# Other start addresses for TensorE's stationary operands, in an attention and expert kernel in split float32

## The chip, the cores and the metric

The kernel runs on one core of one Trainium2 chip. The metric is device time in microseconds from launch to end. The profile is of one further execution; its span runs from the first to the last instruction.

## The reference

The input `x` is 32 sequences of 256 rows of 256 numbers. A bias chosen by an integer per sequence is added to `x` to make the queries; `side` serves as keys and as values:

```python
q = query + braak_embed[braak_stages][..., None]
attn = softmax(einsum('bsd,btd->bst', q, key))
o = einsum('bst,btd->bsd', attn, value)
```

The attention output is normalised by its root mean square and a weight (call it `t`, 8192 rows of 256), and goes through eight experts that share dense weights and differ by low-rank terms. The two best experts of each row count:

```python
h1 = t @ w1.T + SCALING * einsum('etr,efr->etf', t·a1, b1)      # F = 1024, rank 16 per expert
h3 = t @ w3.T + SCALING * einsum('etr,efr->etf', t·a3, b3)
act = silu(h1) * h3
out_e = act @ w2.T + SCALING * einsum(..., act·a2, b2)
out = x + sum over e of weights[t, e] * out_e
```

All of it is float32.

## The kernel before, in words

Float32 products are made of three matmuls. Every operand is split into a high part, a copy rounded to the type float32r, and a low part, what is left; `product` (lines 1190 to 1195) issues high x high, high x low, low x high. A matmul has a stationary operand, which a weight load (PEld in the profile) brings into the array, and a moving one, which streams past it. In `nc.tensor.matmul(dst, w, x)` the first operand, `w`, is stationary and the second, `x`, moving. The profile's names put them the other way round, moving first: `bank<-t_hi,w1T_hi` has `t_hi` moving and `w1T_hi` stationary. Each matmul has its own weight load of 128 columns.

The first stage, up to about 195 us, goes through the 32 sequences one by one: transposes of queries and keys (line 1246, plain fp32, `ident` moving), scores (line 1266 and after: `qT` stationary, `kT` moving, 256 columns), softmax, transposes of the probabilities (line 1297), `attend` (`value` stationary, `probT` moving, 256 columns), and `gate` (line 1319, plain fp32, the same `oT` tile as stationary and moving, 136 columns; its rows are 160 words apart). Between these, `weight_job` (line 1239) transposes the weights, and ScalarE and VectorE write their high and low parts. For `w2_in` and `a2_in` the stationary operand of the transpose takes one word in eight, starting 0 to 7 words in; for the others it is contiguous. The value parts are written by ScalarE (high) and GpSimd (low, line 552), the query and key parts by ScalarE (high) and VectorE (low, lines 857 and 859).

The second stage takes 16 tiles of 512 rows, each in eight chunks of 128 of the F = 1024 columns. Of a tile `pe_tile` (line 1440) issues `low_rank` (`a13T` stationary, 12 matmuls), and by chunk `first_expert` (18: `w1T`, `w3T`, `b1T`, `b3T` stationary), `second_expert` (6: `b1T`, `b3T`), `down_z` (6: `a2T`), all with 512 columns moving. `down_y` (12 per chunk: the activation parts `s` stationary, `w2T` moving) and `finish_y` (12 per tile: `z` stationary, `b2T` moving) have 256 columns. In a tile other than the first the order is low_rank, second_expert, down_z, first_expert, first_expert, second_expert, down_z, first_expert, then down_y twice and finish_y. The order is written out by hand, and semaphores join the engines.

SBUF tensors are laid one behind another in the order in which they are made (lines 72 to 175); `early` ones share their space with the late ones. Two pads, `pad_w` of 352 words and `pad_t` of 304, set where the rest begins. The size of all tensors between `ident` and the small vectors is a multiple of 512 bytes, and so is that of every large tensor of both stages, so all parts of the split operands start on multiples of 512 bytes.

Of the kernel before, what the change touches and what calls it, by code (L numbers as in the profile page):

```python
# [25 lines left out]
F32R = mybir.dt.float32r  # L26
# [5 lines left out]
P = 128  # L32
BATCH, S, D = 32, 256, 256
F, E, R = 1024, 8, 16
STAGES = 6
ER = E * R
SC = S // P
DC = D // P
FC = F // P
# [13 lines left out]
def adaln_moe_ffn(nc, x, side, itok, embed, norm_w, w1, w3, w2, gate_w, a1, b1, a3, b3, a2, b2, out):  # L53
    ctx = ExitStack()
    with ctx:
# [6 lines left out]
        def sb(stack, name, shape, dt=F32):  # L62
            return stack.enter_context(nc.sbuf_tensor(name, shape, dt))
# [7 lines left out]

        sb(ctx, "pad_w", [P, 352])
        ident = sb(ctx, "ident", [P, P])
        def split(name, shape, stack=ctx):
            return sb(stack, name + "_hi", shape, F32R), sb(stack, name + "_lo", shape, F32R)

        w1T = split("w1T", [P, DC, F])
        w3T = split("w3T", [P, DC, F])
        w2T = split("w2T", [P, FC, D])
        a2T = split("a2T", [P, FC, ER])  # L80
        a13T = split("a13T", [P, DC, 2, ER])
        b1T = split("b1T", [ER, F])
        b3T = split("b3T", [ER, F])
        b2T = split("b2T", [ER, D])
        rank_key = sb(ctx, "rank_key", [P, E])
        stage_id = sb(ctx, "stage_id", [STAGES, 1])
        gateT = sb(ctx, "gateT", [P, DC, E])
# [25 lines left out]

        rt = [sb(ctx, f"rt{k}", [P, KT]) for k in range(2)]

        sb(ctx, "pad_t", [P, 304])
        O_STRIDE = P + 32
        GATE = slice(P, P + E)
        early = ExitStack()
# [11 lines left out]
        x_in = [sb(early, f"x_in{k}", [P, SC, D]) for k in range(RING)]  # L131
        kv = [sb(early, f"kv{k}", [P, SC, D]) for k in range(RING)]
        q = [sb(early, f"q{k}", [P, SC, D]) for k in range(2)]
        qT = [split(f"qT{k}", [P, DC * S], early) for k in range(2)]
        kT = [split(f"kT{k}", [P, DC * S], early) for k in range(2)]
        prob = [sb(early, f"prob{k}", [P, SC, S]) for k in range(2)]
        value = [split(f"value{k}", [P, SC, D], early) for k in range(2)]
        probT = [split(f"probT{k}", [P, SC * S], early) for k in range(2)]
        oT = [sb(early, f"oT{k}", [P, DC, SC, O_STRIDE]) for k in range(2)]
        gram_diag = sb(early, "gram_diag", [P, SC, P])  # L140
        embed_in = sb(early, "embed_in", [STAGES, S])
# [1372 lines left out]
```

## Time and profile before

| | |
|---|---|
| median of 3 runs | 1311.74 us (1311.71 to 1311.76) |
| the profiled execution | 1313.57 us |
| its span | 1311.8 us |
| matmuls busy | 1304.6 us, 99% of the span, 7278 instructions |
| weight loads busy | 1143.5 us, 87% |
| VectorE / ScalarE / GpSimd busy | 844.0 / 527.0 / 250.0 us |
| granted TensorE clock | 1.00 |

A matmul's busy time in these views is its latency from start to modelled end, and the next starts before that end. The rate of a stream of matmuls is read from their starts. A weight load is shown with its own start and length. A line "x4" in the order of time merges four instructions that follow each other; its start is that of the first.

### The profile page before, as it was taken

To read this page: it belongs to the slowest core of one execution; us is meant where nothing else is said; L and a number is where in the kernel's file an instruction comes from. 1 tells how busy PE (TensorE), PEld (TensorE's weight loads), DVE (VectorE), ACT (ScalarE), POOL (GpSimd) and SP (SyncE) were. 2 spreads that over 40 slices of the span, in tenths; PEclk is the share of its full clock that TensorE was granted. 3 is DMA by queue.
4 is the path that set the end of the run, shared out by engine and by line. 5 is a ranking of instruction groups with operands and counts; after the bars stand their busy time and mean duration, and the time that the engine had idled before them with its cause. 6 is when DMAs were issued, how large, how long until landed. Compare 5 with 4: busy or idle time off the path is not lost.

```text
span 1311.8 us, 18591 instructions
## 1 busy us (share of the span) xinstructions
PE 1304.6 (99%) x7278; PEld 1143.5 (87%) x7278; DVE 844.0 (64%) x1558; ACT 527.0 (40%) x991; POOL 250.0 (19%) x213
## 2 busy tenths in 40 slices
PE   8999999999999999999999999999999999999998
PEld 8999998888888888888888888888888888888887
DVE  6776656756666576656675577557675666565556
ACT  6776653333343333333343334333333343243332
POOL 2656640202011020202020202011020202020200
PEclk9999999999999999999999999999999999999999
DMA  9454810020202020101102020202020101102000
GB/s 293 133 157 147 228 56 33 2 72 1 73 2 73 1 73 1 58 17 28 47 2 73 1 72 2 73 0 73 2 72 1 57 17 34 41 1 72 0 17 16
DMA packets 73583, 69.56 MB, mean 53 GB/s; under 512 B 7050, under 2 KB 64792, under 8 KB 73368
## 3 DMA queue, kind: packets, MB, share of 16 engines
q1 hardware_dynamic: 72924, 68.11, 17.2%
q8 instruction: 57, 0.93, 0.3%
q10 hardware_dynamic: 572, 0.28, 0.1%
q14 instruction: 30, 0.25, 0.1%
HBM read 51.27 MB, written 17.10 MB: 52 GB/s over the span
## 4 chain that ended last, share of the span: by engine, by line
PE 98%; ACT 1%; DVE 1%; DMA 0%; issue 0%; ACTq 0%; DVEq 0%
PE bank L1193 31%; PE bank L1194 31%; PE bank L1195 31%; PE bank L1319 2%; PE bank L1246 2%; PE bank L1297 1%; PE bank L1239 1%; DMA kv<-in_fside_BxSxS 0%; ACT prob L654 0%; PE bank L1284 0%; ACT kT_hi L638 0%; ACT qT_hi L637 0%; DVE q L850 0%; DVE x_out L1137 0%; PE bank L1326 0%
## 5 line engine op out<-in xcount | busy, mean ns | idle before, releaser
L1065 DVE TENSOR_TENSOR act_a<-silu_a,bank 128x512 f32<-128x512 f32 x128 | 87.6, 685 | 212.4 <-PE bank L1195 195.8
L745 ACT ACTIVATE br_hi<-act_br 128x512 fp32r<-128x512 f32 x128 | 80.9, 632 | 188.4 <-DVE act_br L1076 188.4
L738 ACT ACTIVATE silu_b<-bank 128x512 f32<-128x512 f32 x128 | 76.2, 596 | 187.9 <-PE bank L1195 187.1
L581 POOL TENSOR_TENSOR t_lo<-t_in,t_hi 128x512 fp32r<-128x512 f32 x32 | 40.6, 1290 | 553.2 <-ACT t_hi L725 553.2
L1193 PE MATMUL bank<-w2T_hi,s_hi 128*128 128x256 f32 x512 | 145.2, 284 | 0.0
L1195 PE MATMUL bank<-w2T_hi,s_lo 128*128 128x256 f32 x512 | 145.0, 283 | 0.0
L1194 PE MATMUL bank<-w2T_lo,s_hi 128*128 128x256 f32 x512 | 144.9, 283 | 0.0
L1073 DVE TENSOR_TENSOR act_b<-silu_b,bank 128x512 f32<-128x512 f32 x128 | 87.9, 687 | 81.6 <-PE bank L1195 80.6
L734 ACT ACTIVATE silu_a<-bank 128x512 f32<-128x512 f32 x128 | 75.7, 591 | 135.4 <-PE bank L1195 135.3
L600 POOL TENSOR_TENSOR v_lo<-v_full,v_hi 128x512 fp32r<-128x512 f32 x64 | 94.5, 1510 | 137.2 <-ACT v_hi L730 137.2
L1086 DVE TENSOR_TENSOR br_lo<-act_br,br_hi 128x512 fp32r<-128x512 f32 x128 | 104.7, 818 | 5.6 <-ACT br_hi L745 3.1
L1080 DVE TENSOR_TENSOR act_s<-act_a,act_br 128x512 f32<-128x512 f32 x128 | 103.2, 806 | 4.4
L1193 PE MATMUL bank<-t_hi,w1T_hi 128*128 128x512 f32 x256 | 100.2, 391 | 0.0
L1193 PEld LDWEIGHTS bank<-w2T_hi,s_hi 128*128 128x128 f32 x512 | 98.1, 192 | 2.4
L1194 PE MATMUL bank<-t_lo,w1T_hi 128*128 128x512 f32 x256 | 100.0, 391 | 0.0
L1076 DVE TENSOR_TENSOR act_br<-act_b,rho 128x512 f32<-128x512 f32 x128 | 97.2, 759 | 4.4
L1194 PEld LDWEIGHTS bank<-w2T_lo,s_hi 128*128 128x128 f32 x512 | 98.1, 192 | 2.2
L1193 PE MATMUL bank<-v_hi,b1T_hi 128*128 128x512 f32 x256 | 99.8, 390 | 0.0
L1194 PE MATMUL bank<-v_lo,b1T_hi 128*128 128x512 f32 x256 | 99.7, 390 | 0.0
L1194 PE MATMUL bank<-v_lo,b3T_hi 128*128 128x512 f32 x256 | 99.7, 390 | 0.0
L1193 PE MATMUL bank<-v_hi,b3T_hi 128*128 128x512 f32 x256 | 99.7, 389 | 0.0
L1195 PE MATMUL bank<-v_hi,b1T_lo 128*128 128x512 f32 x256 | 99.7, 389 | 0.0
(197 smaller groups left out, 3255.9 us busy)
## 6 DMA issues: line engine op xcount, KB each, us to landing
x_in<-in_x SPq DMA_DIRECT2D x32, 256.0 KB, 3.7
t_scratch<-oT SPq DMA_DIRECT2D x32, 256.0 KB, 2.5
t_in<-t_scratch SPq DMA_DIRECT2D x16, 512.0 KB
x_out<-in_x SPq DMA_DIRECT2D x16, 512.0 KB, 3.9
kv<-in_fside_BxSxS SPq DMA_DIRECT2D x31, 256.0 KB, 3.4
out<-x_out SPq DMA_DIRECT2D x30, 256.0 KB, 3.9
rho<-scale_scratch SPq DMA_DIRECT2D x16, 256.0 KB
rstd<-scale_scratch SPq DMA_DIRECT2D x16, 256.0 KB
```

The costliest lines, as they stand in the source:

```text
L600: nc.gpsimd.tensor_tensor(v_lo[k][:, :], v_full[k][:, :], f32(v_hi[k][:, :]), ALU.subtract).then_inc(v_lo_ready, 1)
L734: nc.scalar.activation(silu_a[j % 2][:, :], h1_bank[j % 2][:, :], ACT.Silu).then_inc(silu_a_ready, 1)
L738: nc.scalar.activation(silu_b[:, :], h1_bank[j % 2][:, :], ACT.Silu).then_inc(silu_b_ready, 1)
L745: nc.scalar.activation(br_hi[j % 2][:, :], act_br[j % 2][:, :], ACT.Copy).then_inc(br_hi_ready, 1)
L1065: nc.vector.tensor_tensor(act_a[j % 2][:, :], silu_a[j % 2][:, :], h3_bank[j % 2][:, :], ALU.mult).then_inc(act_a_ready, 1)
L1073: nc.vector.tensor_tensor(act_b[:, :], silu_b[:, :], h3_bank[j % 2][:, :], ALU.mult).then_inc(act_b_ready, 1)
L1076: nc.vector.tensor_tensor(act_br[j % 2][:, :], act_b[:, :], rho[c % 2][:, :], ALU.mult).then_inc(act_br_ready, 1)
L1080: nc.vector.tensor_tensor(act_s[j % 2][:, :], act_a[j % 2][:, :], act_br[j % 2][:, :], ALU.add).then_inc(act_s_ready, 1)
L1086: low = nc.vector.tensor_tensor(br_lo[j % 2][:, :], act_br[j % 2][:, :], f32(br_hi[j % 2][:, :]), ALU.subtract)
L1193: nc.tensor.matmul(dst, w_hi, x_hi, start=start, stop=False, skip_group_check=not grouped)
L1194: nc.tensor.matmul(dst, w_hi, x_lo, start=False, stop=False, skip_group_check=not grouped)
L1195: return nc.tensor.matmul(dst, w_lo, x_hi, start=False, stop=stop, skip_group_check=not grouped)
```

## The change

It puts gaps of 8 to 80 words ahead of the high and low parts of the stationary operands and takes 256 words from the second pad. `split` gets a parameter for the gap ahead of each part. No instruction, wait or transfer is added or taken away.

```diff
--- before.py
+++ after.py
@@ -71,17 +71,22 @@
 
         sb(ctx, "pad_w", [P, 352])
         ident = sb(ctx, "ident", [P, P])
-        def split(name, shape, stack=ctx):
-            return sb(stack, name + "_hi", shape, F32R), sb(stack, name + "_lo", shape, F32R)
-
-        w1T = split("w1T", [P, DC, F])
-        w3T = split("w3T", [P, DC, F])
-        w2T = split("w2T", [P, FC, D])
-        a2T = split("a2T", [P, FC, ER])
-        a13T = split("a13T", [P, DC, 2, ER])
-        b1T = split("b1T", [ER, F])
-        b3T = split("b3T", [ER, F])
-        b2T = split("b2T", [ER, D])
+        def split(name, shape, stack=ctx, gaps=(0, 0)):
+            parts = []
+            for part, words in zip(("_hi", "_lo"), gaps):
+                if words:
+                    sb(stack, name + part + "_gap", [P, words])
+                parts.append(sb(stack, name + part, shape, F32R))
+            return tuple(parts)
+
+        w1T = split("w1T", [P, DC, F], gaps=(8, 8))
+        w3T = split("w3T", [P, DC, F], gaps=(8, 24))
+        w2T = split("w2T", [P, FC, D], gaps=(80, 0))
+        a2T = split("a2T", [P, FC, ER], gaps=(64, 8))
+        a13T = split("a13T", [P, DC, 2, ER], gaps=(8, 8))
+        b1T = split("b1T", [ER, F], gaps=(8, 8))
+        b3T = split("b3T", [ER, F], gaps=(8, 8))
+        b2T = split("b2T", [ER, D], gaps=(8, 0))
         rank_key = sb(ctx, "rank_key", [P, E])
         stage_id = sb(ctx, "stage_id", [STAGES, 1])
         gateT = sb(ctx, "gateT", [P, DC, E])
@@ -113,7 +118,7 @@
 
         rt = [sb(ctx, f"rt{k}", [P, KT]) for k in range(2)]
 
-        sb(ctx, "pad_t", [P, 304])
+        sb(ctx, "pad_t", [P, 48])
         O_STRIDE = P + 32
         GATE = slice(P, P + E)
         early = ExitStack()
@@ -131,11 +136,11 @@
         x_in = [sb(early, f"x_in{k}", [P, SC, D]) for k in range(RING)]
         kv = [sb(early, f"kv{k}", [P, SC, D]) for k in range(RING)]
         q = [sb(early, f"q{k}", [P, SC, D]) for k in range(2)]
-        qT = [split(f"qT{k}", [P, DC * S], early) for k in range(2)]
-        kT = [split(f"kT{k}", [P, DC * S], early) for k in range(2)]
+        qT = [split(f"qT{k}", [P, DC * S], early, ((8, 8), (16, 16))[k]) for k in range(2)]
+        kT = [split(f"kT{k}", [P, DC * S], early, ((80, 0), (0, 0))[k]) for k in range(2)]
         prob = [sb(early, f"prob{k}", [P, SC, S]) for k in range(2)]
-        value = [split(f"value{k}", [P, SC, D], early) for k in range(2)]
-        probT = [split(f"probT{k}", [P, SC * S], early) for k in range(2)]
+        value = [split(f"value{k}", [P, SC, D], early, ((64, 16), (24, 8))[k]) for k in range(2)]
+        probT = [split(f"probT{k}", [P, SC * S], early, ((16, 0), (0, 0))[k]) for k in range(2)]
         oT = [sb(early, f"oT{k}", [P, DC, SC, O_STRIDE]) for k in range(2)]
         gram_diag = sb(early, "gram_diag", [P, SC, P])
         embed_in = sb(early, "embed_in", [STAGES, S])
```

## Rows read from the trace of the kernel before

**Rows 1.** The page's first part: busy us, share of the span, instructions.

```profile
PE 1304.6 (99%) x7278; PEld 1143.5 (87%) x7278; DVE 844.0 (64%) x1558; ACT 527.0 (40%) x991; POOL 250.0 (19%) x213
```

**Rows 2.** The page's fourth part: the chain by engine, then by line.

```profile
PE 98%; ACT 1%; DVE 1%; DMA 0%; issue 0%; ACTq 0%; DVEq 0%
PE bank L1193 31%; PE bank L1194 31%; PE bank L1195 31%; PE bank L1319 2%; PE bank L1246 2%; PE bank L1297 1%; PE bank L1239 1%; DMA kv<-in_fside_BxSxS 0%; ACT prob L654 0%; PE bank L1284 0%; ACT kT_hi L638 0%; ACT qT_hi L637 0%; DVE q L850 0%; DVE x_out L1137 0%; PE bank L1326 0%
```

**Rows 3.** Stretches: us, busy us (count) by engine, clock, DMA share, GB/s.

```profile
30.00:195.00 165.00, 164.93 (x1369) 162.32 (x1369) 108.76 (x317) 113.19 (x286) 94.34 (x90) 1.00 0.51 149
195.00:1307.00 1112.00, 1112.00 (x5722) 955.20 (x5721) 714.73 (x1197) 396.21 (x667) 146.92 (x105) 1.00 0.11 32
```

**Rows 4.** Matmuls in order of time: start us, us, engine, line, operands.

```profile
878.24 0.40 PE L1193 MATMUL bank<-t_hi,a13T_hi 128*128 128x512 f32 x1
...
898.67 0.28 PE L1193 MATMUL bank<-w2T_hi,s_hi 128*128 128x256 f32 x1
```

**Rows 5.** The same view from 902.98 us, and one weight load (PEld).

```profile
902.98 0.40 PE L1193 MATMUL bank<-v_hi,b1T_hi 128*128 128x512 f32 x1
...
903.45 0.39 PE L1195 MATMUL bank<-v_hi,b1T_lo 128*128 128x512 f32 x1
...
904.37 0.39 PE L1193 MATMUL bank<-s_hi,a2T_hi 128*128 128x512 f32 x1
...
902.98 0.19 PEld L1194 LDWEIGHTS bank<-v_lo,b1T_hi 128*128 128x128 f32 x1
```

**Rows 6.** Weight loads of transposes and gate in order of time.

```profile
126.66 0.47 PEld L1246 LDWEIGHTS bank<-ident,kv 128*128 128x128 f32 x4
127.09 1.00 PEld L1319 LDWEIGHTS bank<-oT 128*128 128x128 f32 x8
128.02 0.19 PEld L1193 LDWEIGHTS bank<-probT_hi,value_hi 128*128 128x128 f32 x1
```

**Rows 7.** Matmul groups by form, with their counts and mean latency.

```profile
L1193 PE MATMUL bank<-w2T_hi,s_hi 128*128 128x256 f32 x512 | 145.2, 284 | 0.0
...
L1193 PE MATMUL bank<-t_hi,w1T_hi 128*128 128x512 f32 x256 | 100.2, 391 | 0.0
...
L1193 PE MATMUL bank<-br_hi,a2T_hi 128*128 128x512 f32 x128 | 49.8, 389 | 0.0
...
L1193 PE MATMUL bank<-probT_hi,value_hi 128*128 128x256 f32 x128 | 39.0, 304 | 0.0
L1193 PE MATMUL bank<-kT_hi,qT_hi 128*128 128x256 f32 x124 | 37.5, 303 | 0.0
...
L1193 PE MATMUL bank<-t_hi,a13T_hi 128*128 128x512 f32 x64 | 25.2, 394 | 0.0
```

**Rows 8.** Groups of weight loads, and two groups that write the parts.

```profile
L1193 PEld LDWEIGHTS bank<-w2T_hi,s_hi 128*128 128x128 f32 x512 | 98.1, 192 | 2.4
...
L1193 PEld LDWEIGHTS bank<-v_hi,b1T_hi 128*128 128x128 f32 x256 | 48.1, 188 | 9.6
...
L552 POOL TENSOR_TENSOR value_lo<-kv,value_hi 128x512 fp32r<-128x512 f32 x32 | 41.4, 1293 | 80.4 <-ACT value_hi L648 80.4
...
L857 DVE TENSOR_TENSOR qT_lo<-bank,qT_hi 128x512 fp32r<-128x512 f32 x31 | 21.4, 691 | 16.3 <-ACT qT_hi L637 16.1
```

**Rows 9.** `w2_in` loads (first) and `w1_in`, `w3_in` ones; then in order.

```profile
L1239 PEld LDWEIGHTS bank<-ident,w_in x16: 186/189/193, 35.2 to 44.8; 128*128 128x128 f32 x16
...
L1239 PEld LDWEIGHTS bank<-ident,w_in x12: 139/140/142, 26.4 to 32.8; 128*128 128x128 f32 x12
...
38.47 0.53 PEld L1239 LDWEIGHTS bank<-ident,w_in 128*128 128x128 f32 x4
38.91 0.19 PEld L1193 LDWEIGHTS bank<-kT_hi,qT_hi 128*128 128x128 f32 x1
...
29.16 0.47 PEld L1239 LDWEIGHTS bank<-ident,w_in 128*128 128x128 f32 x4
29.60 0.42 PEld L1319 LDWEIGHTS bank<-oT 128*128 128x128 f32 x3
```

## Prediction

> **What bounds the kernel now.** I read the busy shares first: TensorE's matmuls fill 99% of the span and no other engine more than 64% [rows 1]. The matmuls' mean in such a row is a latency, since one starts before the last has ended, so "busy" alone says little. The chain of waits decides: 98% of the chain that ends last is TensorE, 93% of it the three lines of `product` [rows 2]. The stretches say the same: from 195 to 1307 us the matmuls are busy for all 1112.00 us, from 30 to 195 us for 164.93 of 165.00 [rows 3]. The granted clock is 1.00 throughout, which is the 2.4 GHz level. So the time is the number of matmuls times the interval from one start to the next, and only that interval can move the result by more than a microsecond or two.
>
> I took the interval from the order of time. Between the first low-rank matmul at 878.24 and the first `w2T` one at 898.67 lie 90 matmuls of 512 columns (12 of low_rank, 54 of three first_expert, 12 of two second_expert, 12 of down_z): 20.43 / 90 = 227.0 ns. Between 898.67 and 902.98 lie 36 of 256 columns (24 of two down_y, 12 of finish_y): 4.31 / 36 = 119.7 ns [rows 4, 5]. The difference of 107.3 ns for 256 columns is 0.419 ns a column, one column a cycle of 2.4 GHz. What is left over, 227.0 - 214.5 = 12.5 ns, is a fixed part of every matmul in this format, in which a weight load of its own runs each time.
>
> The plain fp32 matmuls have less of it. Four `kv` transposes take 127.09 - 126.66 = 0.43 us, eight gate matmuls 128.02 - 127.09 = 0.93 us by the starts of their weight loads, 108 and 116 ns each [rows 6]. They take two cycles a column (8 columns more cost 8 ns): 128 x 0.838 = 107 ns, so their fixed part is about 1 to 2 ns. About 11 ns of the 12.5 is thus particular to the split format. No row says if it is a fixed step or two reads that get in each other's way. That is the whole stake of this change.
>
> **The change part by part.** It adds and removes no instruction, no wait and no DMA; it moves addresses. Adding up the gaps in words (8 words are 32 bytes): `w1T` parts start 32 and 64 bytes off, `w3T` 96 and 192, `a2T` 256 and 288, `a13T` 320 and 352, `b1T` 384 and 416, `b3T` 448 and 480, `qT` 32, 64, 128, 192, `value` 256, 320, 416, 448. `w2T`, `b2T`, `kT`, `probT` and all the loop's operands (`t`, `v`, `s`, `br`, `z`) stay on 512. The gaps of the weights sum to 1024 bytes and the second pad gives up 1024, so everything behind it starts where it did.
>
> Counting by the groups [rows 7]: twelve groups of 256 with `w1T`, `w3T`, `b1T`, `b3T` as stationary (3072), 768 with `a2T`, 192 with `a13T`: 4032 matmuls of 512 columns. With `qT` and `value` 768 of 256 columns. 4800 of 7278 matmuls get another stationary start. Not touched: 1536 with `s` as stationary, 192 with `z`, and the 750 or so in plain fp32.
>
> The sum before: 4032 x 227.0 = 915.3 us; (1728 + 768) x 119.7 = 298.8 us; the other 98 us are transposes, gate, the start and the end, which keep their addresses' remainders or run in fp32. The 915.3 us are what a change of the interval acts on: each nanosecond on every shifted 512-column matmul is 4.0 us, each on the shifted 256-column ones 0.8 us.
>
> Step one, the load itself. Its cover among 512-column matmuls: it starts with the matmul before it and lasts 188 ns of the 227 [rows 5, 8], so 39 ns are free. If a start off 512 makes it read one piece more, it may lengthen by some part. The nearest row for a stationary read in a worse pattern are the `w2_in` transposes: there one column in eight words is taken, starting 0 to 28 bytes past a multiple of 512. These loads last 189 ns against 140 for the contiguous ones, yet four of them take 38.91 - 38.47 = 0.44 us, as the contiguous four do (29.60 - 29.16 = 0.44) [rows 9]. 49 ns more of load cost nothing there within the 10 ns of the rows, at most 2 ns a matmul. Without the cover (256 columns: 192 ns of load at an interval of 119.7, each load starting as the matmul before it starts) I bound it by 0 and the same 2 ns: 768 x 2 = 1.5 us. Below nothing: the fixed part could fall, which is a rival below. I take 0.
>
> Step two, the stationary read against the moving read. What speaks for no effect: the stationary slices already stand at many different multiples of 512 (`w1T[:, c, f]` walks 512 bytes a chunk) against moving rows of 2048 bytes, and the 90 matmuls keep 227 ns over three chunks; plain fp32 gate reads start 0, 128, 256 and 384 bytes off 512 (row stride 640 bytes), and hold 116 ns. But in the gate the moving operand starts at the very same address, so the difference of the two is always nothing, and it reads at half rate. Neither row has what the change makes: a full-rate moving read on 512 beside a stationary one off it. I take 0 here too, since a read of 2048 bytes passes every remainder of 512 four times during one load, wherever that load began.
>
> Of this the Trainium skill has two rules. The page "SBUF — State Buffer" says under "Who interferes with whom" that TensorE has two independent read ports, one for each operand, and waits on no one; by it the change is worth nothing, and no row contradicts it, though the 11 ns have no place in it. The page "TensorE: Matmul & The Clock Gate" gives under "Back-to-back issue gap" columns / 2.4 + 2.5 ns for a warm matmul: 215.8 ns for 512 columns, where the rows show 227.0.
>
> Step three, the engines that write these parts. ScalarE's, VectorE's and GpSimd's instructions on `qT_lo` (691 ns) or `value_lo` (1293 ns) write to shifted starts [rows 8]. They run while TensorE is busy 164.93 of 165.00 us [rows 3]; without that cover, 1% of the 31 x 0.691 + 32 x 1.293 = 63 us would be 0.6 us. I take 0.
>
> The sum is 0 on the profiled execution's 1313.57 us (span 1311.77 and 1.80 around it). The median of the runs shown is 1311.74, 1.83 below that, and it is the base: 1311.7 us.
>
> **The rivals.**
> - *Slower: the two reads stop falling into step.* After each run of 256-column matmuls the 512-column ones don't take 227 ns at once: the six from 902.98 to 904.37 take 1.39 us, 231.7 ns each, the first two 903.45 - 902.98 = 0.47 us, 235 each. They then settle [rows 5]. Their count, kind and operands' size are the same; what differs is how the load and the matmul stand to each other. That is evidence that the interval depends on it. If shifted starts keep the stream in the unsettled pattern, the price is 4032 x 4.7 = 19.0 us, 1330.7; with the first two's 8 ns it is 32.3 us, 1344.0. It decides from 0.65 ns a matmul on (2.6 us, 0.2%). Against it: the stream settled within six matmuls by itself. The 256-column ones have no such pattern, so I leave them at nothing.
> - *Faster: the 11 ns are a clash of equal remainders.* Now every load and every moving read start at the same remainder of 512, within 10 ns of each other. If that is what costs, shifted loads shed up to 11 ns: 4032 x 11 = 44.4 us and 768 x 11 = 8.4 us, 1258.9; half of it is 1285.3. For it: fp32, with half the read rate, lacks the 11 ns. By the TensorE page's formula (the Trainium skill, same section) a 512-column matmul would reach 215.8 ns, 45 us less in all. Against it: the moving read passes each remainder of 512 again after 128 columns, so an equal start alone should not bind the two for a whole load; and the 256-column matmuls, whose read is half as long, pay the same 12 to 13 ns.
> - *The edit moves nothing that counts*: the tensors could be placed on another grain than words, but the gaps are multiples of 32 bytes; this gives the forecast's time and is inside it.
>
> **How the numbers follow.** No change within 0.2% (2.6 us, about what a measurement tells from nothing): 0.46, at 1311.7 with its own range 1310 to 1314. Slower: 0.36, most of it at 1316 to 1331 since only some remainders may be bad ones, little at 1344. Faster: 0.18, spread from 1309 down to 1259, half of it above 1290. The range from 1296 to 1335 leaves out about 0.06 above and 0.11 below. These three cases are all, so the chances are theirs.
>
> **What would show it.** Right: the stretch from the first low-rank matmul to the first `w2T` one is again 20.43 us, its loads 188 ns. Slower by the first rival: that stretch grows (20.85 us for 4.7 ns), the loads there last 192 instead of 188 ns, and 36 matmuls with `s` and `z` as stationary still take 4.31 us. Faster: it shrinks towards 19.4 us, the 36 unchanged. If only some remainders matter, the interval differs by tensor within one chunk: `w1T`'s against `b1T`'s. Wrong altogether would be a change in the 36, or in the span before 195 us while the rest stands.

## The result, and the profile after

The changed kernel takes 1332.15 us (median of 4, 1331.61 to 1332.46) against 1311.72: 20.4 us slower. The ratio of the fast runs is 1.0151 on record, interval 1.0139 to 1.0163 (the two medians alone give 1.0156, inside it). The profiled execution took 1332.05 us with a span of 1330.3.

The page of the kernel after, busy us and shares, and the long stretch of the second stage (us, busy us and count by engine, clock, DMA share, GB/s):

```profile
PE 1323.5 (99%) x7278; PEld 1142.3 (86%) x7278; DVE 844.6 (63%) x1558; ACT 527.2 (40%) x991; POOL 250.3 (19%) x213
...
194.00:1325.00 1131.00, 1131.00 (x5717) 954.25 (x5715) 714.96 (x1197) 396.09 (x666) 147.04 (x105) 1.00 0.11 32
```

Counts are those of [rows 1]; TensorE is again busy for the whole stretch at the same clock, as in [rows 3], and the other engines' busy time is the same within a microsecond. The same instructions run without a wait, only each further from the last. The second stage, from the first low-rank matmul to the end, takes 1151.3 us by the trace where the kernel before took 1131.4: 20.0 us more. The matmuls' starts in order of time, from the first low-rank matmul of the tile of [rows 4] to the first `w2T` one and on to the first after finish_y:

```profile
889.13 0.40 PE L1198 MATMUL bank<-t_hi,a13T_hi 128*128 128x512 f32 x1
...
910.02 0.28 PE L1198 MATMUL bank<-w2T_hi,s_hi 128*128 128x256 f32 x1
...
914.33 0.39 PE L1198 MATMUL bank<-v_hi,b1T_hi 128*128 128x512 f32 x1
```

The 90 matmuls of 512 columns take 20.89 us, 232.1 ns each, against 20.43 us and 227.0 [rows 4]. The 36 with `s` and `z` as stationary, which the change does not touch, take 4.31 us, as before [rows 4, 5]. 5.1 ns on 4032 matmuls is 20.6 us, the whole loss of the medians (20.4 us). The two spans differ by 18.5 us only, since the profiled execution of the kernel before was 1.8 us slower than its median. By form (mean latency is the number before the last bar) the loss differs from tensor to tensor:

```profile
L1199 PE MATMUL bank<-v_lo,b1T_hi 128*128 128x512 f32 x256 | 101.6, 397 | 0.0
...
L1199 PE MATMUL bank<-br_lo,a2T_hi 128*128 128x512 f32 x128 | 51.1, 400 | 0.0
...
L1200 PE MATMUL bank<-br_hi,a2T_lo 128*128 128x512 f32 x128 | 50.1, 391 | 0.0
```

All three stood at 389 or 390 ns before (the groups with `a2T_hi`, `a2T_lo` and `b1T_hi` were alike within 1 ns); now they are 400, 397 and 391. The slowest of them, `a2T_hi`, starts 256 bytes past 512, which the experiments below show to cost nothing by itself; so a matmul's latency in this mixture does not depend on its own distance alone. The weight loads did not get longer, 188 ns here as in [rows 8]:

```profile
L1198 PEld LDWEIGHTS bank<-v_hi,b1T_hi 128*128 128x128 f32 x256 | 48.1, 188 | 10.8
```

### The profile page after: what moved, and what is told of

It is laid out like the page before. It is cut to its first block, busy times and chain, and to the rows that moved or that the text cites. A ratio compares the mean times of both kernels' runs of the same rounds, so it can differ in the third digit from the quotient of the medians.

```text
span 1330.3 us, 18591 instructions
## 1 busy us (share of the span) xinstructions
PE 1323.5 (99%) x7278; PEld 1142.3 (86%) x7278; DVE 844.6 (63%) x1558; ACT 527.2 (40%) x991; POOL 250.3 (19%) x213
## 4 chain that ended last, share of the span: by engine, by line
PE 98%; ACT 1%; DVE 1%; DMA 0%; issue 0%; ACTq 0%; DVEq 0%
PE bank L1199 31%; PE bank L1198 31%; PE bank L1200 30%; PE bank L1324 2%; PE bank L1251 2%; PE bank L1302 1%; PE bank L1244 1%; ACT prob L659 0%; DMA kv<-in_fside_BxSxS 0%; ACT qT_hi L642 0%; ACT kT_hi L643 0%; PE bank L1289 0%; DVE q L855 0%; DVE probT_lo L882 0%; DVE x_out L1142 0%
## 5 line engine op out<-in xcount | busy, mean ns | idle before, releaser
L1198 PE MATMUL bank<-t_hi,w3T_hi 128*128 128x512 f32 x256 | 101.2, 395 | 0.0
L1199 PE MATMUL bank<-t_lo,w3T_hi 128*128 128x512 f32 x256 | 100.8, 394 | 0.0
L1200 PE MATMUL bank<-v_hi,b3T_lo 128*128 128x512 f32 x256 | 100.7, 393 | 0.0
L1200 PE MATMUL bank<-t_hi,w3T_lo 128*128 128x512 f32 x256 | 100.7, 393 | 0.0
```

What stands on the lines that cost most here:

```text
L1198: nc.tensor.matmul(dst, w_hi, x_hi, start=start, stop=False, skip_group_check=not grouped)
L1199: nc.tensor.matmul(dst, w_hi, x_lo, start=False, stop=False, skip_group_check=not grouped)
L1200: return nc.tensor.matmul(dst, w_lo, x_hi, start=False, stop=stop, skip_group_check=not grouped)
```

## The experiments

In the comparisons below the kernel before ran again beside each batch, at 1312.4 to 1312.6 us. Three theories stood at first. *Own place* (A in the expectations): a read that starts off a multiple costs by itself. *Distance* (B): what counts is the start of the stationary operand less that of the moving one, modulo some period. *Variety* (C): what counts is that successive loads begin at different remainders. Later expectations name a fourth, F: a fixed step of every float32r matmul, with a penalty for a start off 256.

**map: matmuls alone.** The kernel keeps only a stream of matmuls and ran once, as did the two later maps; letters a to p stand for remainders 0, 32, ... 480. Its core, written short:

```python
for m in (0, 32, 128, 256):            # moving mv_a, mv_b, mv_e, mv_i
    for o in range(0, 512, 32):        # stationary st_a ... st_p
        for k in range(24):
            matmul(bank[n % 2], st[o][:, k % 4 * 128:(k % 4 + 1) * 128], mv[m], start=True, stop=True)
```

> A kernel of matmuls alone (it leaves the computation out): streams of 24 float32r matmuls, 128x128 stationary and 128x512 moving, for each of 16 stationary remainders (0 to 480 bytes past 512 in steps of 32) and 4 moving remainders (0, 32, 128, 256), then 8 streams whose loads alternate between two remainders. Theory A (own place: a load or a read that starts off 512 costs by itself): stationary 0 at 227 ns for moving 0, the 15 others 230 to 236. Theory B (relative: the distance between the two remainders counts): 227 ns wherever the two are equal, (32,32), (128,128) and (256,256) too, slower elsewhere. Theory C (variety: it is the change of remainder from one load to the next that unsettles the stream): every stream of one remainder at 227, only the alternating ones at 230 or more.

In order of time, 24 matmuls to a row (fewer in a last row, where the view's window ends); the interval is the difference of two rows' starts over 24. The first rows have the moving operand on 512, the next 32 bytes past it, the last 128:

```profile
30.47 5.75 PE L69 MATMUL bank<-mv_a,st_b 128*128 128x512 f32 x24
36.06 5.76 PE L69 MATMUL bank<-mv_a,st_c 128*128 128x512 f32 x24
...
52.87 5.76 PE L69 MATMUL bank<-mv_a,st_f 128*128 128x512 f32 x24
58.48 5.67 PE L69 MATMUL bank<-mv_a,st_g 128*128 128x512 f32 x24
63.98 5.76 PE L69 MATMUL bank<-mv_a,st_h 128*128 128x512 f32 x24
69.58 5.61 PE L69 MATMUL bank<-mv_a,st_i 128*128 128x512 f32 x24
75.03 5.75 PE L69 MATMUL bank<-mv_a,st_j 128*128 128x512 f32 x24
...
119.73 5.64 PE L69 MATMUL bank<-mv_b,st_b 128*128 128x512 f32 x24
125.21 5.75 PE L69 MATMUL bank<-mv_b,st_c 128*128 128x512 f32 x24
...
219.96 5.76 PE L69 MATMUL bank<-mv_e,st_d 128*128 128x512 f32 x24
225.55 5.61 PE L69 MATMUL bank<-mv_e,st_e 128*128 128x512 f32 x24
231.00 1.32 PE L69 MATMUL bank<-mv_e,st_f 128*128 128x512 f32 x5
```

Distance 32 (`mv_a,st_b`): 5.59 us, 232.9 ns; distance 192 (`st_g`) 5.50 us, 229.2; distance 256 (`st_i`) 5.45 us, 227.1. Equal remainders at 32 (`mv_b,st_b`) 5.48 us, 228.3 with the first few unsettled; at 128 (`mv_e,st_e`) 5.45 us, 227.1. Once settled (the last 18 of each stream, by the starts in the trace) every pair follows one table of the distance modulo 256: 0: 226.7 ns; 32, 64, 128, 160, 224: 233.3; 96: 234.1; 192: 228.9; it repeats at distance 256 and for all four moving places but for one stream just after a change of moving operand. Loads that alternate between two distances lie elsewhere: 0 and 256 at 226.6, 0 and 32 at 235.0, 32 and 64 at 231.0, 384 and 416 at 233.2, 32 and 256 at 230.0; the changed kernel's mixture at 232.1 is among them. As an estimate, this table weighted by the distances of the changed kernel's 90 matmuls gives 232.1 ns, and 226.7 for the kernel before, where 232.1 and 227.0 were measured. The sum comes out, though its single terms need not: loads that alternate between 0 and 32 take 235.0, not the 230.0 halfway between the two. Own place falls (a load 32 or 128 bytes off runs at 227 beside a moving operand as far off), variety falls as the sole cause (a constant 32 costs 6.6 ns).

**s32, s256, both256: the same in the kernel.** All moved stationary parts on one remainder, 32 or 256 bytes past 512, or every tensor behind the first pad 256 bytes on.

```diff
 # s32, against the changed kernel (s256 has 64 for 8 and for 120)
-        w1T = split("w1T", [P, DC, F], gaps=(8, 8))
-        w3T = split("w3T", [P, DC, F], gaps=(8, 24))
-        w2T = split("w2T", [P, FC, D], gaps=(80, 0))
-        a2T = split("a2T", [P, FC, ER], gaps=(64, 8))
+        w1T = split("w1T", [P, DC, F], gaps=(8, 0))
+        w3T = split("w3T", [P, DC, F])
+        w2T = split("w2T", [P, FC, D], gaps=(120, 0))
+        a2T = split("a2T", [P, FC, ER], gaps=(8, 0))
 # a13T, b1T, b3T without gaps; b2T, kT, probT with 120; qT, value with 8
 # both256, against the kernel before
-        sb(ctx, "pad_w", [P, 352])
+        sb(ctx, "pad_w", [P, 288])
```

> All the stationary parts that the change moved start at the same remainder, 32 bytes past 512; moving parts on 512. A (own place): every load is off, 1325 to 1335 us. B (relative): the distance is 32 everywhere, 1320 to 1335. C (variety): one common remainder, so 1311.7, as before.

> The same with 256 bytes past 512. A (own place): 1325 to 1335 if the grain is 512 bytes, 1312 if it is 256 or finer. B (relative): other than before, 1320 to 1335, if the period is 512; 1312 if it is 256 or less. C (variety): 1311.7.

> The first pad is 64 words smaller, so every tensor behind it, stationary and moving, starts 256 bytes past 512. A (own place): loads and reads are off, at least the changed kernel's loss, 1325 to 1340. B (relative): all distances are 0 again, 1311.7. C (variety): 1311.7.

s32: 1335.88 us, ratio 1.0182 (1.0165 to 1.0199). s256: 1312.32, ratio 1.0000 (0.9991 to 1.0009). both256: 1312.51, the same ratio. The first two rows are s32, the others s256's:

```profile
890.69 0.40 PE L1198 MATMUL bank<-t_hi,a13T_hi 128*128 128x512 f32 x1
...
911.68 0.28 PE L1198 MATMUL bank<-w2T_hi,s_hi 128*128 128x256 f32 x1
```

```profile
876.98 0.40 PE L1198 MATMUL bank<-t_hi,a13T_hi 128*128 128x512 f32 x1
...
897.41 0.28 PE L1198 MATMUL bank<-w2T_hi,s_hi 128*128 128x256 f32 x1
```

90 matmuls take 20.99 us (233.2 ns) and 20.43 us (227.0). One common remainder costs even more than the changed kernel's mixture, so variety as the cause is out; 256 bytes cost nothing in the kernel either, so a period of 256 bytes holds there too, and both256, which leaves all distances at 0 as well, could not part the theories.

**both32, s192, mov32.** Every tensor 32 bytes on; the stationary parts at 192; the loop's operands 32 bytes on with the weights left on 512.

```diff
 # both32, against the kernel before
-        sb(ctx, "pad_w", [P, 352])
+        sb(ctx, "pad_w", [P, 232])
 # mov32, against the kernel before
-        sb(ctx, "pad_t", [P, 304])
+        sb(ctx, "pad_t", [P, 184])
 # s192: as s32, with 48 for 8 and 80 for 120
```

> The first pad is 120 words smaller: every tensor behind it, stationary and moving, starts 32 bytes past 512. Theory A (own place, grain 256 or finer): 1335 us, as when the stationary parts alone stood there, or more. Theory B (distance): 1312.5, as before.

> The stationary parts all 192 bytes past 512, moving parts on 512. Theory B by the first map: 228.9 - 226.7 = 2.2 ns on 4032 matmuls, 8.9 us more, 1321. Theory A (any start off 256 costs): 1335, as with 32 bytes.

> The second pad is 120 words smaller: the loop's tensors (t, v, s, br, z) and the first stage's big ones start 32 bytes past 512, while all the stationary weights stay on 512. The distance in the 4032 matmuls is -32, 224 mod 256. Theory B (distance) with the maps: 233.3 - 226.7 = 6.6 ns on each, 26.6 us more, 1339; s and z against w2T and b2T come to +32, 118.3 instead of 120, 2.9 us less; together 1336. Theory A' (only a weight load's own start counts): the loads of the weights are all on 512, so 1312.

both32: 1313.57 us, ratio 1.0011 (1.0002 to 1.0020). s192: 1319.87, ratio 1.0055 (1.0038 to 1.0071), 7.4 us more where the map promised 8.9; its 90 matmuls are 228.9 ns apart by the starts in the trace. mov32: 1336.54, ratio 1.0181 (1.0165 to 1.0197), 24.1 us more, with 26.6 - 2.9 us expected. In both32 all starts are off and the loop's interval is unchanged:

```profile
878.36 0.40 PE L1193 MATMUL bank<-t_hi,a13T_hi 128*128 128x512 f32 x1
...
898.78 0.28 PE L1193 MATMUL bank<-w2T_hi,s_hi 128*128 128x256 f32 x1
```

That is 20.42 us by these rows, 20.43 as the mean of the 15 tiles like it, 227.0 ns. In mov32 no weight has moved, and the loss is there; its 36 matmuls of 256 columns get shorter, 4.25 us for 4.31:

```profile
893.24 0.39 PE L1193 MATMUL bank<-t_hi,a13T_hi 128*128 128x512 f32 x1
...
914.23 0.28 PE L1193 MATMUL bank<-w2T_hi,s_hi 128*128 128x256 f32 x1
...
918.48 0.39 PE L1193 MATMUL bank<-v_hi,b1T_hi 128*128 128x512 f32 x1
```

20.99 us again, 233.2 ns. Distance modulo 256 is shown from both sides. The 0.1% of both32 is not in the second stage: from its first low-rank matmul to the end the traces of the kernel before, s256, both256 and both32 all have 1131.4 us. It lies ahead of that, where both32 takes 180.5 us and the other three 179.1 to 180.4; its cause there is open.

**map2: other lengths and formats.** The same streams (the core above with other lists), moving operand on 512, with 256 and 384 columns, with fine distances (`fine_b`, `_c`, `_e`, `_g`, `_m`: 4, 8, 16, 24, 48 bytes), with loads of 32 to 96 columns, in plain fp32 (`plain_a`, `_b`, `_e`: 0, 32, 128) and in bfloat16 (`half_a` on).

> Matmuls alone again (the computation is left out), moving operand always on 512: float32r with 256, 512 and 384 columns against 8 stationary distances of 0 to 224 bytes and 5 fine ones (4, 8, 16, 24, 48 bytes), then loads of 32, 64 and 96 columns at distances 0 and 32, plain fp32 with 256 columns at 0, 32, 128, and bfloat16 with 512 columns at 0 to 224. Theory B (distance mod 256, two reads that meet in the same place of the memory): the 512-column table repeats (226.7; 233.3 for most; 228.9 at 192), shorter loads pay a smaller fixed part in proportion (32 columns: 4 ns instead of 13), plain fp32 and bfloat16, which read at half the rate, show no distance at all. Theory F (a fixed step of a float32r matmul plus a penalty for a start off 256): short loads keep the 13 ns. For 256 columns, where the load is exposed, the first map says nothing; the changed kernel's qT and value streams had 112 to 118 ns beside 120, so I expect some distances at 116 to 118 and 0 at 120.

```profile
33.81 2.99 PE L79 MATMUL bank<-mv_a,st_c 128*128 128x256 f32 x24
36.64 2.98 PE L79 MATMUL bank<-mv_a,st_d 128*128 128x256 f32 x24
...
53.67 2.94 PE L79 MATMUL bank<-mv_a,fine_c 128*128 128x256 f32 x24
56.44 3.01 PE L79 MATMUL bank<-mv_a,fine_e 128*128 128x256 f32 x24
...
192.00 5.73 PE L79 MATMUL bank<-mv_a,st_a 128*32 128x512 f32 x24
197.56 5.87 PE L79 MATMUL bank<-mv_a,st_b 128*32 128x512 f32 x24
203.27 5.69 PE L79 MATMUL bank<-mv_a,st_a 128*64 128x512 f32 x24
...
225.37 10.52 PE L79 MATMUL bank<-plain_mv,plain_a 128*128 128x256 f32 x48
235.73 10.52 PE L79 MATMUL bank<-plain_mv,plain_b 128*128 128x256 f32 x48
246.09 10.52 PE L79 MATMUL bank<-plain_mv,plain_e 128*128 128x256 f32 x48
256.45 5.34 PE L79 MATMUL bank<-half_mv,half_a 128*128 128x512 bf16 x24
261.63 5.34 PE L79 MATMUL bank<-half_mv,half_b 128*128 128x512 bf16 x24
266.81 5.34 PE L79 MATMUL bank<-half_mv,half_c 128*128 128x512 bf16 x24
```

With 256 columns distance 64 takes 2.83 us for 24, 117.9 ns; 8 bytes 2.77 us, 115.4; distance 0, settled, 120.0. Loads of only 32 columns take 5.56 us at distance 0 (231.7 ns) and 5.71 us at 32 (237.9): the fixed part does not shrink with the load, so my picture of a toll on each piece that the load reads is wrong. With loads of 96 columns the order even turns: 5.52 us (230.0 ns) at distance 0, 5.50 (229.2) at 32. So the table holds for loads of 128 columns. Plain fp32, whose 24 matmuls the trace shows as 48, takes 10.36 us for 48 of 256 columns at each of its three distances, bfloat16 5.18 us for 24 of 512 at each of its eight, both 215.8 ns: none of these distances counts, and the 11 ns are gone. That is the 215.8 of the Trainium skill's page "TensorE: Matmul & The Clock Gate", "Back-to-back issue gap". The page calls its formula the gap of an isolated matmul and gives a shorter one for a stream; here the formula's figure is the interval of the bfloat16 stream, and of the plain fp32 one if two cycles are counted for a column, and not that of float32r.

**map3: all 64 distances in steps of 4 bytes.** The core is that of the first map with `range(0, 256, 4)` and one moving operand, first with 256 columns, then 512. Names carry two letters, the first for steps of 32 bytes, the second for steps of 4 (`st_cb` stands at 68).

> Matmuls alone (the computation is left out): float32r, moving operand on 512, stationary at all 64 distances of 0 to 252 bytes in steps of 4, streams of 24 with 256 columns, then with 512. Theory B (distance mod 256): 512 columns best at 0 with 226.7 ns, nothing below it; steps of 4 bytes vary it between 227 and 234. 256 columns: 0 gives 120, 8 gives 115.6 and 96 gives 117.2 again, and no distance gives the 109 ns of columns / 2.4 + 2.5, since the second map had none below 115.6. Theory F (a start off 256 costs a fixed step): two values only, one for 0 and one for all others.

With 512 columns 226.6 or 226.7 ns is the lowest, at 0, 120, 132, 144, 156, 204, 228 and 252 bytes; all others lie between 228.3 and about 237. Expected were 227 to 234. With 256 columns distance 64 now gave 113.3, where the second map had 117.8:

```profile
94.81 2.89 PE L70 MATMUL bank<-mv_a,st_ca 128*128 128x256 f32 x24
97.54 2.65 PE L70 MATMUL bank<-mv_a,st_cb 128*128 128x256 f32 x21
```

2.73 us for 24, 113.8 ns with the first ones. Distance 96 gave 118.9 where the second map had 117.2, and five distances stood at 113.3, below the second map's lowest, 115.6. The same distance can settle into more than one pattern, and distance alone does not fix the 256-column interval.

**w96, w64, w8: a faster version.** The 512-column matmuls keep distance 0 modulo 256; `w2T` and `b2T`, and `kT` and `probT`, are moved so that their stationary partners stand 96, 64 or 8 bytes ahead.

```diff
 # w64, against the changed kernel (w96 has 40 for 48, 24 for 16, a pad of 200)
+        w1T = split("w1T", [P, DC, F])
+        w3T = split("w3T", [P, DC, F])
+        w2T = split("w2T", [P, FC, D], gaps=(48, 0))
+        a2T = split("a2T", [P, FC, ER], gaps=(16, 0))
+        b2T = split("b2T", [ER, D], gaps=(48, 0))
+        sb(ctx, "pad_t", [P, 192])
 # a13T, b1T, b3T without gaps; kT, probT with 48; qT, value with 16
 # w8, against the kernel before: high and low parts are views of one tensor, from that word on
+        w2T = packed("w2T", [P, FC, D], 62)[0]
+        b2T = packed("b2T", [ER, D], 62)[0]
+        qT = packed("qT", [P, DC * S], 2, 2, early)
+        value = packed("value", [P, SC, D], 2, 2, early)
```

> A version meant to be faster: the 4032 matmuls of 512 columns keep distance 0; w2T and b2T (moving) move to 160 bytes past 256, so that s and z stand 96 bytes ahead of them, and qT and value 96 bytes ahead of kT and probT. Theory B with the second map: 117.2 instead of 120.0 ns on 1728 + 768 matmuls of 256 columns, 7 us less, 1305.4 beside 1312.4. Theory A (any start off 256 costs by itself): slower than before, since 2496 operands are now off. If the loop's mix of high and low parts unsettles it: 1309 to 1312.

> As the version with 96 bytes, but s, z, qT and value 64 bytes ahead of their moving operands. The second map had 117.8 ns for this distance, the third 113.3: the stream has more than one pattern into which it can fall. Theory B: between 2.2 and 6.7 ns less on 2496 matmuls, 5.5 to 16.7 us at most; the version with 96 bytes got a third of what its map promised (119.2 instead of 117.2), so I expect 1307 to 1311 beside 1312.5.

> The same with 8 bytes, set inside larger tensors. Both maps had 115.5 to 115.6 ns, the only distance below 116 in both. Theory B: at most 4.4 ns on 2496 matmuls, 11 us, 1301.5; if the mix of high and low parts keeps only a third, 1309.

w96: 1309.97 us, ratio 0.9979 (0.9970 to 0.9988). w64: 1305.86, ratio 0.9949 (0.9937 to 0.9962), 6.6 us faster than the kernel before. w8: 1310.88, ratio 0.9988 (0.9979 to 0.9997). w96 and w8 fell short of what the maps promised (1305.4 and 1301.5), and w64 did better than the 1307 to 1311 expected. In w64:

```profile
872.34 0.39 PE L1198 MATMUL bank<-t_hi,a13T_hi 128*128 128x512 f32 x1
...
892.74 0.28 PE L1198 MATMUL bank<-w2T_hi,s_hi 128*128 128x256 f32 x1
...
896.98 0.39 PE L1198 MATMUL bank<-v_hi,b1T_hi 128*128 128x512 f32 x1
```

The 36 take 4.24 us instead of 4.31 (117.8 ns) and the 90 take 20.40 us instead of 20.43. The six matmuls behind each finish_y, which took 231.3 ns on average, now take 226.7 from the first on. The second stage is 4.8 us shorter than in s256 (1126.6 for 1131.4): 1728 x 2 ns is 3.5 us of it, and the 512-column matmuls give most of the rest. The time ahead of the first low-rank matmul gives the other 1.8 us; there the settled 256-column intervals average 115.1 ns by the starts in the trace, for 119.5 in s256. w8's distance was the only one below 116 ns in both maps, and it gained least: its 36 stay at 4.32 us, 120.0 ns. The streams of the maps have one stationary tensor and one moving one, the kernel alternates high and low parts. Whether that is the reason, and why 64 bytes do better than 8, stays open.

## Why the prediction was wrong

The forecast was no change (0.46), with the range 1296 to 1335. The 1332.15 lies in that range because the slower rival was given its room, not because the forecast was near: no change was forecast, and the kernel is 1.5% slower.

- **The bound** was read rightly: the time is the matmuls' interval, no wait appeared, and the sum's count (4032 matmuls, 4.0 us per nanosecond) turns the measured 5.1 ns into 20.6 us.
- **Step one, the load itself**: 0, and that held. The loads stay at 188 ns.
- **Step two, "I take 0 here too, since a read of 2048 bytes passes every remainder of 512 four times during one load"**, is the step that failed. It treats the two reads as unrelated. The maps show that the settled interval goes with their starting distance: 226.7 ns at 0, 233.3 at most other multiples of 32. The term was 5.1 ns a matmul in the changed kernel, 20.6 us, and not 0. The two rows that I took as evidence could not show it. The `w1T` slices are all at multiples of 512, two whole periods, and the gate is plain fp32, in which no distance tried in map2 counts. I had noted of the gate that neither row "has what the change makes" and then gave the silence weight.
- **The `w2_in` transposes** [rows 9] could not show it either: their operands are plain fp32.
- **Step three, the writing engines**: 0, held within the 1 us of their busy times.
- **The slower rival** was right in place and near in price: 4.7 ns from the unsettled pattern of [rows 5] gave 1330.7; 5.1 ns and 1332.15 were measured. Those six matmuls were the one row of the trace before in which the standing of load and matmul differed, and the best evidence in it. I discounted them because the stream settles by itself; at other distances it settles too, on a slower interval. The signature was half right: the stretch of 90 grew to 20.89 us and the 36 stood still, but the loads did not go to 192 ns.
- **The faster rival**, equal remainders as a clash, is refuted: among the 64 distances of map3 none is under 226.6 ns with 512 columns. But its other half had something: with 256 columns distance 0 is one of the slower ones, which w64 turned into 0.5%.
- **The first stage**: I bounded the `qT` and `value` matmuls by 0 to +1.5 us and left "below nothing" to the rival. They got faster, 118.3 ns on average where distance 0 has 119.5, about 1 us. It is not visible in the time up to the first low-rank matmul: 178.9 us, where the four traces with all distances at 0 modulo 256 have 179.1 to 180.5.
- **The rule of the Trainium skill** that TensorE's two read ports wait on no one ("SBUF — State Buffer", "Who interferes with whom") does not foretell what float32r showed: s32 and mov32 cost 6.2 ns a matmul, both32 nothing, and what parts them is the distance of the two reads. Whether the ports are where it costs, no run shows. With plain fp32 and bfloat16 no distance showed, as the rule has it.

What stays open: what in the chip has the period of 256 bytes; why 120, 132 and five other distances with 512 columns are as good as 0; why even the best distance costs 11 ns more than the other formats, also with a load of 32 columns; and why one distance can settle in two ways.

## What to carry to other kernels

In a stream of float32r matmuls, keep stationary and moving operands at the same remainder of 256 bytes when the moving side has 512 columns and the load 128: a common distance of 32 bytes cost this TensorE-bound one 1.8%, and it is the distance that counts, not the alignment to anything. With 256 columns try other distances, in the kernel itself, since a map with one pair of tensors does not carry over to a mix. A row with another format or the same distance says nothing on a question of distance; where the trace before is silent on what a change makes, a short stream of that instruction alone answers it in one run.

## What the runs showed of the hardware that I had not expected

- A float32r matmul's interval depends on the distance of its two SBUF operands modulo 256 bytes, with loads of 128 columns: 226.7 to about 237 ns with 512 columns, 113.3 to 123.3 with 256; plain fp32 and bfloat16 stand at 215.8 ns at each distance tried.
- A load of 32 columns makes a float32r matmul of 512 columns no faster than one of 128, rather slower: 231.7 against 227 ns at distance 0, 237.9 against 233 at 32.
- With 384 columns the interval at distance 0 and at 32 is the same, 173.3 ns settled, and at 128 it is 176.3: columns and distance act together.
